# A graph network on one Trainium2 core: adjacency counts packed in four classes of eight-destination columns instead of two of four, and the late in-degree counts moved to ScalarE's queue, behind the last unpacking

## What is computed

```python
def sage(x):                                   # twice, with relu between
    msg = x[src]
    agg = segment_sum(msg, dst)                # = adjacency counts @ x
    cnt = segment_sum(ones, dst)               # in-degree of each node
    return (agg / maximum(cnt, 1)) @ W_l.T + b_l + x @ W_r.T

def mp_layer(h):                               # three times, self loops added
    m = concatenate([h[dst_f], h[src_f], ea_f], 1) @ W.T + b
    return relu(segment_sum(m, dst_f))         # batchnorm + relu behind the first two

x = layernorm(x + sage_stack(x))
x = layernorm(x + mp_stack(x))
```

## Time and profile before

| | us |
|---|---|
| Median of three runs | 1078.5 |
| Lowest, highest | 1074.97, 1079.38 |
| Profiled execution, its own time | 1073.11 |
| Profiled execution, span of the trace | 1071.3 |
| TensorE, busy | 923.9 (86%) |
| VectorE, busy | 686.6 (64%) |
| ScalarE, busy | 406.3 (38%) |
| POOL, busy | 131.8 (12%) |

### The profile page before, as it was taken

How to read it: one execution, slowest core, us unless ns; L and a number is a source line. 1 busy time by engine, 2 the same in 40 slices (tenths; PEclk the granted TensorE clock), 3 DMA queues, 4 the chain that set the end, 5 groups by cost and what they waited for, 6 DMA issues and landing times. The chain is left out here.

```text
span 1071.3 us, 19165 instructions
## 1 busy us (share of the span) xinstructions
PE 923.9 (86%) x7566; PEld 566.3 (53%) x7566; DVE 686.6 (64%) x1288; ACT 406.3 (38%) x847; POOL 131.8 (12%) x150
## 2 busy tenths in 40 slices
PE   0357877979788778999999999997999997999995
PEld 0356776878687765545555544444444444444443
DVE  6898989999999954624433756655395456332334
ACT  2684788888888821100000010104411022401113
POOL 4212313244232320000000000000000000000001
PEclk9868989889899998999999999998999998999998
DMA  6735546756665497964774607776018775037771
GB/s 145 182 97 183 190 137 196 254 160 197 197 207 173 125 338 234 364 247 150 306 312 184 251 22 301 305 266 258 16 33 324 290 281 242 10 115 289 270 282 31
DMA packets 65160, 218.63 MB, mean 204 GB/s; under 512 B 28986, under 2 KB 42891, under 8 KB 51523
## 3 DMA queue, kind: packets, MB, share of 16 engines
q1 hardware_dynamic: 55444, 164.26, 43.2%
q0 software_dynamic: 9616, 53.04, 14.5%
HBM read 170.43 MB, written 45.22 MB: 201 GB/s over the span
## 5 line engine op out<-in xcount | busy, mean ns | idle before, releaser
L1462 PE MATMUL PM<-Aring,Xop 128*128 128x512 fp8e4 (+1 forms) x1960 | 396.7, 363 | 2.3 <-issue 2.3
L1462 PEld LDWEIGHTS PM<-Aring,Xop 128*128 128x128 f16 x1960 | 182.3, 98 | 214.1 <-issue 11.3
L1462 PE MATMUL PM<-Ares,Xop 128*128 128x512 fp8e4 x588 | 136.4, 387 | 2.7 <-ACT Xop L2074 1.2
L1836 DVE TENSOR_SCALAR S<-PM 128x256 f32<-128x256 f32 x72 | 30.6, 424 | 153.2 <-PE PM L1462 64.8
L929 PE MATMUL PM<-Aring 128*128 128x104 fp8e4 (+3 forms) x1616 | 95.2, 217 | 35.1 <-ACT F L998 35.0
L2025 ACT ACTIVATE F<-PH,bag 64x512 f32<-64x512 f32 (+1 forms) x39 | 25.7, 659 | 260.8 <-PE PH L1679 260.3
L929 PEld LDWEIGHTS PM<-Aring 128*128 128x128 fp8e4 x1616 | 85.7, 103 | 38.1 <-ACT F L998 36.9
L1462 PEld LDWEIGHTS PM<-Ares,Xop 128*128 128x128 f16 x588 | 56.0, 99 | 70.1 <-issue 7.3
L1592 POOL DMA_DIRECT2D out<-hT x12 | 9.0, 754 | 652.1 <-DVE hT L1793 652.1
L786 DVE TENSOR_TENSOR Aring<-Ares 128x4096 uint16<-128x4096 uint16 x31 | 70.9, 2287 | 4.9 <-PE PW L929 4.6
L998 ACT ACTIVATE F<-PM 128x392 uint16<-128x392 f32 x147 | 66.6, 516 | 6.7 <-PE PM L929 5.4
(11 more groups left out here) (170 smaller groups left out, 1265.6 us busy)
## 6 DMA issues: line engine op xcount, KB each, us to landing
Aring<-adj SPq DMA_DIRECT2D x72, 1568.0 KB, 9.8
adj<-Aring POOLq DMA_DIRECT2D x12, 1568.0 KB, 7.0
adj<-Xop POOLq DMA_DIRECT2D x12, 1568.0 KB, 6.8
Ares<-adj SPq DMA_DIRECT2D x6, 1568.0 KB, 20.2
rc<-ea_sum SPq DMA_DIRECT2D x36, 128.0 KB, 6.6
Aring<-adj SPq DMA_DIRECT2D x4, 784.0 KB, 4.6
rc<-rc_d SPq DMA_DIRECT2D x12, 256.0 KB, 9.7
eaf<-in_erow SPq DMA_DIRECT2D x60, 51.0 KB, 2.1
```

What stands on the lines that cost most here:

```text
L1462: last = nc.tensor.matmul(o, x[:, h, :], rhs, start=h == 0, stop=h == NT - 1)
L1836: own(nc.vector.tensor_single_scalar(part, of, 1 / CS, ALU.mult))
```

## The change

From stage 1 on eight destinations share a column instead of four: each byte holds four classes of two bits (mask 0x0303), the values added are 1, 4, 16 and 64. Stage 0, the densest, stays as it was. Slots, turns, banks and tables follow from the planner's new numbers: 1840 slots instead of 1983, 29 turns instead of 31, 15 tables instead of 16, 102 banks instead of 196 (a bank of 64 destinations has the columns that 32 had), and 1922 slot matmuls instead of 2151. The key products are 114 with 85124 elements a partition instead of 139 with 105820; one digit's masks change. An unpacked stage takes four operations of 1568 elements instead of two of 3136. The packed stages have five places (`NHOME`) at the upper end of `F` instead of four, so `xT` is loaded in three pieces. There are 30 chunks of attributes as before, for 29 turns: turns 14 and 28 have two, turn 0 none, and `high(c)` of a chunk whose buffer is that of a chunk of the turn before is moved behind the evacuations and sums.

The classes of the in-degrees are now eight: the early counts are loaded and stored in three pieces and summed by three reductions. The late counts are loaded and stored by ScalarE's queue, with a semaphore of their own, behind ScalarE's last work in the build, and VectorE makes them behind the last unpacking instead of ahead of it. Fewer stages are finished in the last turn but one: f = 22 and 23 are unpacked in the last turn (28), ahead of the early counts; f = 24 alone is left for the end. In the layers `sums` writes each class with a stride of four elements (16 bytes) where it wrote pairs, and the lanes are eight of 416 elements instead of four of 832.

```diff
+def unit(d):
+    return d // 4 if d < SW else SW // 4 + (d - SW) // 8
+
+
+def first_of(u):
+    return 4 * u if u < SW // 4 else SW + 8 * (u - SW // 4)
...
-        found.append(((a + min(met)) // 4, (a + max(met)) // 4 - (a + min(met)) // 4 + 1))
+        found.append((unit(a + min(met)), unit(a + max(met)) - unit(a + min(met)) + 1))
...
+    u = 4 if b <= SW else 8
+    for x in range(b - u, a - u, -u):
         options = []
-        for y in range(x + 4, b + 1, 4):
+        for y in range(x + u, b + 1, u):
             w = bands(x, y)
-            if max(q for _, q in w) <= 4:
+            if max(q for _, q in w) <= (4 if u == 4 else 3):
...
-BANK = 32
-BANKS = [cut(a, a + BANK) for a in range(0, NP, BANK)]
+BANKS = [cut(a, a + 32) for a in range(0, SW, 32)] + [cut(a, a + 64) for a in range(SW, NP, 64)]
...
+def stage_of(bank):
+    return 0 if bank < 8 else 1 + (bank - 8) // 4
+
+
+def place_of(bank):
+    return bank if bank < 8 else (bank - 8) % 4
...
+    HOME[_st] = [NHOME - 2, NHOME - 1] if _st == 0 else [min(_users, key=lambda h: _users[h])]
+    assert all(_users[h] < BEGUN[_st] for h in HOME[_st])
...
-GIVEN = [(0, 2), (2, NB)]
+GIVEN = [(0, 4), (4, 7), (7, NB)]
...
-                    there, here = spread(m, "ea_sum", cnt, 0, EARLY)
-                    sp.dma_start(here, there).then_inc(m["s_cl"], 16)
+                    for there, here in early_parts(m, "ea_sum", cnt):
+                        sp.dma_start(here, there).then_inc(m["s_cl"], 16)
+                if c == NCH // 2:
+                    given(sp, ins, m, 0)
...
-            sp.wait_ge(m["s_cr"], 4)
-            there, here = spread(m, "rc_d", cnt, 0, EARLY)
-            sp.dma_start(there, here).then_inc(m["s_cd"], 16)
+            sp.wait_ge(m["s_cr"], 6)
+            for there, here in early_parts(m, "rc_d", cnt):
+                sp.dma_start(there, here).then_inc(m["s_cd"], 16)
             sp.wait_ge(s_pe, NS)
             sp.wait_ge(s_sti, TS + PT)
             products(sp, m, 0)
-            sp.wait_ge(m["s_cd"], 16)
+            sp.wait_ge(m["s_cd"], 48)
             reciprocals(sp, m, 0)
-            sp.wait_ge(s_un, 1 + max(RANK[st] for st in range(NST) if HOME[st] == 0))
-            given(sp, ins, m, 0)
             reciprocals(sp, m, 1)
             products(sp, m, 1)
-            for i in range(2):
-                sp.wait_ge(s_eo[i], 16 * (13 - i))
-            there, here = spread(m, "ea_sum", late, EARLY, NP)
-            sp.dma_start(here, there).then_inc(m["s_cl"], 16)
+            sp.wait_ge(s_un, 1 + max(RANK[st] for st in range(NST) if HOME[st][0] < 2))
+            given(sp, ins, m, 1)
             products(sp, m, 2)
             products(sp, m, 3)
-            sp.wait_ge(m["s_cr"], 8)
-            there, here = spread(m, "rc_d", late, EARLY, NP)
-            sp.dma_start(there, here).then_inc(m["s_cd"], 16)
             sp.wait_ge(s_un, NST)
-            given(sp, ins, m, 1)
+            given(sp, ins, m, 2)
...
-                op(d[:, 3], node, -4, None, ALU.bitwise_and)
-                op(d[:, 4], node, 4, 0x20, ALU.logical_shift_left, ALU.bitwise_and)
-                op(d[:, 5], node, 6, 0x40, ALU.logical_shift_left, ALU.bitwise_and)
+                op(d[:, 3], node, -8, None, ALU.bitwise_and)
+                op(d[:, 4], node, 4, 0x30, ALU.logical_shift_left, ALU.bitwise_and)
+                op(d[:, 5], node, 4, 0x40, ALU.logical_shift_left, ALU.bitwise_and)
...
-                of = packed[:, HOME[st], 0:NT * n // 4].rearrange("p (h a q) -> p a h q", h=NT, a=2)
-                to = stage[f % 2][:, 0:NT * n // 2].rearrange("p (h z a q) -> p z a h q", h=NT, z=2, a=2)
-                nc.vector.tensor_scalar(to[:, 0], of, 0x0F0F, None, ALU.bitwise_and)
-                nc.vector.tensor_scalar(to[:, 1], of, 4, 0x0F0F, ALU.logical_shift_right,
-                                        ALU.bitwise_and).then_inc(s_un, 1)
+                z, mask = (2, 0x0F0F) if st == 0 else (4, 0x0303)
+                to = stage[f % 2][:, 0:NT * n // 2].rearrange("p (h z q) -> p z h q", h=NT, z=z)
+                nc.vector.tensor_scalar(to[:, 0], packed(st), mask, None, ALU.bitwise_and)
+                for i in range(1, z):
+                    last = nc.vector.tensor_scalar(to[:, i], packed(st), 8 // z * i, mask, ALU.logical_shift_right,
+                                                   ALU.bitwise_and)
+                last.then_inc(s_un, 1)
...
-                    v.wait_ge(m["s_cl"], 16)
-                    counts(nc, v, cnt[:], m["csum"][:, 0, :], m["s_cr"], 0)
+                    v.wait_ge(m["s_cl"], 48)
+                    for i in range(2):
+                        nc.vector.tensor_reduce(
+                            m["csum"][:, 0, :].rearrange("p (z f e) -> p f z e", z=2, f=2)[:, i],
+                            cnt[:, 8 * i:8 * i + 8].rearrange("p (q e z) -> p z e q", e=2, z=2), AX.X,
+                            ALU.add).then_inc(m["s_cr"], 1)
+                    classes(nc, cnt[:, SW // 16:EARLY // 16], m["csum"][:, 1, :], m["s_cr"])
+                    counts(nc, v, cnt[:], m["s_cr"], 3)
...
-            for f in unpacked_after(NH)[:-1]:
+            for f in unpacked_after(NH):
                 unpack(f)
-            v.wait_ge(m["s_cl"], 32)
-            counts(nc, v, late, m["csum"][:, 1, :], m["s_cr"], 4)
-            unpack(NST - 1)
+            v.wait_ge(m["s_ld"], 16)
+            classes(nc, late, m["csum"][:, 2, :], m["s_cr"])
+            counts(nc, v, late, m["s_cr"], 7)
...
-                st, o = TURN[g] // 8, TURN[g] % 8 * 8
-                n = stage_width(st) // 4
+                st, o = stage_of(TURN[g]), place_of(TURN[g]) * 8
                 act.wait_ge(s_pe, LAST_OF[g] + 1)
                 if g == BEGUN[st] and BEFORE[st]:
                     act.wait_ge(s_un, BEFORE[st])
-                to = packed[:, HOME[st], 0:NT * n].rearrange("p (h q) -> p h q", h=NT)[:, :, o:o + 8]
-                nc.scalar.activation(to, PW[g % RING][:, 0:416].rearrange("p (q h) -> p h q", h=52)[:, 0:NT], ACT.Copy,
+                nc.scalar.activation(packed(st)[:, :, o:o + 8], PW[g % RING][:, 0:416].rearrange("p (q h) -> p h q", h=52)[:, 0:NT], ACT.Copy,
...
-                if h < NH:
-                    for c in CHUNKS[h]:
-                        high(c)
+                chunks = CHUNKS[h] if h < NH else []
+                before = [c for c in chunks if c - 2 not in CHUNKS[h - 1]]
+                for c in before:
+                    high(c)
...
-                for c in CHUNKS[h] if h < NH else []:
+                for c in chunks:
+                    if c not in before:
+                        high(c)
                     low(c)
...
+            for i in range(2):
+                act.wait_ge(s_eo[i], 16 * (13 - i))
+            there, here = spread(m, "ea_sum", late, EARLY, NP)
+            act.dma_start(here, there).then_inc(m["s_ld"], 16)
+            act.wait_ge(m["s_cr"], 10)
+            there, here = spread(m, "rc_d", late, EARLY, NP)
+            act.dma_start(there, here).then_inc(m["s_ld"], 16)
...
-            sp.wait_ge(m["s_cd"], 32)
+            sp.wait_ge(m["s_ld"], 32)
...
-        def by_quad(x):
-
-            return x.rearrange("p (z q e) -> p q z e", z=2, e=2)
-
-        def natural(x):
-            return x.rearrange("p (q z e) -> p q z e", z=2, e=2)
+        def by_lane(x, z):
+
+            return x.rearrange("p (z m) -> p z m", z=z)
+
+        def natural(x, z):
+            return x.rearrange("p (m z) -> p z m", z=z)
...
-        for i in range(4):
-            x = t["acc"].rearrange("p (h z q) -> p h z q", h=13, z=2)[:, :, i // 2, :].bitcast(u8)
-            if 4 * r + i:
-                act.wait_ge(t["s_rd"], 4 * r + i)
+        for i in range(8):
+            x = t["acc"].rearrange("p (h z q) -> p h z q", h=13, z=4)[:, :, i // 2, :].bitcast(u8)
+            if 8 * r + i:
+                act.wait_ge(t["s_rd"], 8 * r + i)
```

117 lines of the change are left out of this document (66 added, 51 removed).

## The result

| | before | changed |
|---|---|---|
| Median of the runs | 1077.61 (4 runs, 1074.97 to 1079.38) | 1116.16 (4 runs, 1113.64 to 1118.78) |
| Span of the profiled execution | 1071.3 | 1111.8 |
| First large product to the last | 342.1 | 365.6 |
| Last large product to the first layer's matmuls | 34.55 | 47.46 |
| Layers | 666.3 | 669.5 |

Times in us. The median of before is of one run more than the 1078.5 of the first table. The ratio of the changed kernel's time to that of the kernel before is 1.036, with a 95% interval of 1.0326 to 1.0394: slower by 38.6 us, where 7.6 us faster was forecast. Of the 40.5 us between the spans 23.5 lie in the build's loop, 12.9 in its end, 3.2 in the layers and 0.9 ahead of the loop.

What follows compares the result with a forecast made beforehand. VectorE was taken to bound the build, TensorE the layers. Loop -9.3 us (work -24.3, waits +15), end +1.2 and layers +0.5 sum to -7.6, from 1078.5 to 1070.9 us; own range 1064 to 1076.

Steps and rivals of the forecast that it cites:

- VectorE's work, unpacking: Build loop: four operations of 1568 elements at 0.561 us replace two of 3136 at 0.973; +0.9 us in all.
- The rest of VectorE's work: Build loop: large products -4.4 us, keys -12.4, one table fewer -6.6, attributes -2.4; small table edits give back 0.6.
- Waits at pairs: Build loop: two more costly pairs of products in even turns, about 5 us each, between 0.55 and 6.87.
- The two-chunk turns: Build loop, turns 14 and 15: line 828 waits for high halves behind the evacuations, two waits, 5 us.
- The end: Last large product to first layer's matmuls: +35.7 us instead of +34.55, late load taken as 4 us; costs +1.2.
- The layers: Layers: strided sums at most 0.13 us more an operation, mostly hidden, and eight lanes; +0.5 us, bounds 0 and +3.
- The slower rival: End of build: late counts become the chain, load 13.0 us and joinings 2.82 each; about 1085 us, chance 0.08.
- the rivals: Cheap pairs 1060 us (0.15); dear late load 1080 (0.12); TensorE or strided writes 1075 to 1077 (0.10); late counts 1085 (0.08).
- The sign for a loop above 332 us: Build loop: a loop above 332 us would show the forecast wrong, with another engine as the bound.
- The signs of faster and slower: Whole kernel: below 1073.1 us is faster, chance 0.62; above 1083.9 us is slower, chance 0.08.

Runs made afterwards that it cites:

- e1: Changed kernel with each unpacking operation walked as two outer halves of 49 rows of 16, same addresses: 1095.34 us, ratio 1.0193.
- e2: Kernel before with unpacking walked as 49 rows of 64 instead of two outer halves of 49 rows of 32: 1102.62 us, ratio 1.0253.
- e6: On e1: ScalarE takes a pair's first product out ahead of the table's turning round in turns 4, 12 and 20: 1073.09 us, ratio 0.9978.
- e10: Changed kernel with the take's edit of e6 alone, unpacking not split: 1096.46 us, ratio 1.0197.
- e9: Kernel before with the take's edit of e6 alone, for its one such pair in turn 4: 1068.81 us, ratio 0.9941.
- e7: On e1: one attribute chunk in each turn from turn 0 on, two only in the last: 1092.13 us, ratio 1.0143.
- e12: On e11: the first double turn of attribute chunks moved from turn 14 to turn 21: 1062.03 us, ratio 0.9879.
- e4: On e1: POOL joins and stores the last attribute sums ahead of the stores of stages of rank 22 and 23: 1085.49 us, ratio 1.0083.
- e11: Changed kernel with the edits of e1, e4 and e6, and rank 23 unpacked behind early counts, b2 and weights: 1061.86 us, ratio 0.9895.
- e3: On e1: layers write sums as pairs again, to other destinations' places, same number of elements: 1092.34 us, ratio 1.0162.
- e8: On e1: late counts loaded and stored by SP ahead of xT, made ahead of the last unpacking: 1096.53 us, ratio 1.0185.

## Why the prediction was wrong

**VectorE's work, unpacking: the step that failed.** I priced the four new operations by the row with the same number of elements, 0.561, and took +0.9 us for all. They took 0.96. The element count was equal and the walk was not: the changed unpacking writes 49 rows of 32, reads a stage that lies in one run, and has no outer dimension of two. e1 and e2 show both directions, in both kernels. It is 34 us of VectorE's work in the loop: 336.0 us were measured where 325.9 - 24.3 = 301.6 was forecast, and e1 and e6 have 301.9 and 301.7. Of it 22.7 us came off the loop in e1 and 28.5 with the pairs mended (e10 to e6), and 18 to 21 off the time of e1 (by the ratios, by the medians).

The Trainium skill has the rule, on the page "VectorE: DVE Perf Modes", section "What auto-detection actually checks": an operation with one source, source and destination in SBUF, uses both read ports only if the outermost dimensions of the two are both even, or equal. The four cases agree: two outer halves on both sides give 0.558 us for 1568 elements and 0.97 for 3136, and 49 rows on the destination's side 0.96 and 1.78. As written in the program, though, source and destination both have 49 rows, which are equal; that the slow form is taken fits the rule only if the source, whose rows touch, counts as one run. No run here shows that part by itself. The order of both kernels had shown me 128x2x49x32 and 128x49x32 for this operation, and I passed over it.

**The rest of VectorE's work: right.** Large products, keys, tables and attributes fell as worked out. Without the pairs' waits, e6 against e9, the loop is 318.5 against 337.3 us: 18.8 less, where 24.3 less work and 5 us of waits for the two-chunk turns were forecast; measured are 24.1 less work and 5.3 more waits.

**Waits at pairs: the mechanism right, the size too small.** "About 5 us for each" was the term. In the changed kernel three pairs cost 18.6 us (e10), of which before had 4.8 (e9), so two more cost 14 rather than 10. All new waits of VectorE together, 13.4 us, are even below the 15 of the forecast, partly because the slow unpacking fills them. With the unpacking at the price that I had taken, three pairs cost 24.4 us (e6) and two more 19.6: by this, e1's loop is 0.8 us longer than before rather than 9.3 shorter. So the forecast would have failed even with the unpacking at that price: e1's time is 1.019 of the time before. The row of before (4.42 to 6.87) was taken in turn 4. Here the second product waited 10 to 12 us and then ran 2 to 3 us longer, and besides the next large product it held up the evacuations, for which the unpacking waits. In turn 12 VectorE's wait was 8.24 us: the bound of 6.87 was no upper bound. The pair of turn 23 wasn't cheap for TensorE either.

**The two-chunk turns: right.** 5 us of waits were taken; e6 has 5.3 more than e9, and its rows at line 861 show 3.21 and 2.37 us for the high halves. In e1 5.34 us for edges come on top, and with the pair's stall they go (e6). The 7.4 us of e7 and 6.6 of e12 hold 2.4 us of work of the chunk that was moved.

**The end: wrong, +12.9 instead of +1.2.** The chain was the one described, and its pieces longer: the unpacking of rank 23 3.7 us instead of 2.2, the product of rank 21 at +14.4 instead of +12, the last joining issued at +31.3 instead of +26.2 (3.25 us beside `b2` and not 1.14), 6.4 us to land instead of 2.4, the load 6.7 instead of 4. The 2.4 were taken from a store of the same size that POOL issued 0.27 us ahead of SP's loads of `rc_d` (384.39 and 384.66); here two such loads were issued 0.8 and 0.4 us ahead of it. The 1568 KB store of rank 23 had landed by then, so it was not what held the small one up. e4, which brings the small stores ahead of SP's loads, lands the last in 1.63 us and takes 6 us off the end; e11, where they fall behind the loads again, has 6.4 and 6.3 us. All fourteen profiles divide this way: 1.6 to 2.5 us where the store was issued ahead of the loads of `rc_d` (before, e4, e9), 6.1 to 8.3 in the other eleven. No run moved the loads alone, so the cause is read from this order and not shown by itself. ScalarE's load did go past some of SP's: issued at 432.51 it landed at 439.2, ahead of two loads of `s` that SP had issued at 427.82 and 428.65 and that landed at 443.8 and 445.3. It took 6.7 us all the same. The slower rival had this mechanism, with the load at 13.0; by itself it would have stayed near 1085.

**The layers: +3.2 instead of +0.5, just above the bound of +3.** The sums cost 604 ns, 180 more, where I had at most 130, taken from rows of another operation, type and source. But e3 takes those 180 ns back without making the layers shorter, so they are not the cause. Three profiles of kernels with the old layers' code gave 664.4 to 667.3 us, eleven with the new one (e3's pairs among them) 667.3 to 671.0: on the mean 3 us more, with ranges that touch. Whether the eight lanes, the longer telling or the order of the loads makes these 3 us was not tried and stays open.

**Which rival, which sign.** None of the rivals had the unpacking. The sign for a loop above 332 us was "another engine is the bound", and it misled: the loop took 358.1 us by that count and VectorE was its bound, with more work than before. The signs of faster and slower were set by costs that I had taken from neighbouring rows without asking whether the new instruction has the same form.

## What to carry to other kernels

An operation is priced by a row of its own form: not only engine, type and element count, but how many outer dimensions source and destination have and with what counts (49 rows against two halves here). Rewriting a walk over the same bytes with an outer dimension of two gave back 0.4 us of 0.96. When two products share one PSUM bank, put the read-out of the first ahead of the long copies on its engine: that one piece of order was worth 22 us beside e1, 18 to 20 in the changed kernel, and 7 in the kernel before. A small store at the head of a chain belongs ahead of the large loads that it does not need. And when work falls on the busiest engine, look at once for turns in which the others have two things to do.

## What was not expected of the hardware

- A walk of 49 rows instead of two halves of 49 rows doubles the time per element of a VectorE operation from SBUF to SBUF on 16-bit data: 0.97 to 1.78 us for 3136 elements, 0.56 to 0.96 for 1568.
- Writing 256 f32 from PSUM with one element in every 16 bytes took 604 ns, with two 424. The Trainium skill, page "SBUF — State Buffer", section "Door 1: The DMA port swizzle (why [64,N] ≈ [32,N])", says that each access that goes on to a new line costs, and also that strides of up to four f32 are free. The trace agrees with the first: this stride is not free.
- A product of 49 matmuls that came behind a wait of TensorE of 10 to 12 us took 7.48 and 8.32 us instead of 5.51. The granted clock during these products was 0.73 and 0.65 of full speed, means between the levels of 1.2 and 2.4 GHz; during the product of e6 that waited 0.55 us and took 5.51 (169.85 to 175.36) it was 1.00.
- A 16.5 KB store by POOL landed in 2.4 us, and in 1.63 in e4, when SP's loads of `rc_d` were issued behind it, and in 6.43 us in the changed kernel (6.1 to 8.3 in ten others) when these loads, of 0.5 and 1 MB, had been issued 0.4 to 3 us ahead of it.
- A 10.5 KB load took 13.0 us and 4.57 (e8) on SP's queue, both times landing 0.2 us behind the load ahead of it, and 5.3 to 6.9 us on ScalarE's queue in the ten kernels that use it.
